# Decoder layer in one launch: the residual of cross attention's output put into the bank by TensorE for the halved batches, statistics and scaling read from the bank, and the last third put in another order

## The chip, the cores and the metric

The kernel runs on one core of one Trainium2 chip. The metric is the device time of one execution in microseconds, smaller is better. Engines are named as in the profile: PE is TensorE's matmul, PEld its weight load, DVE is VectorE, ACT is ScalarE, POOL is GpSimd, SP is SyncE, which issues the DMAs. "Bank" is one of the eight accumulator banks, 512 fp32 columns wide, that PE writes.

## The reference

The layer is a decoder block with the norm behind each residual. The input `x` is (4, 512, 128), the context (4, 77, 128), all fp32:

```python
x = _layernorm(x + _L0_attn_ref(x, ...))            # causal self attention, 16 heads of 64
x = _layernorm(x + _L0_xattn_ref(x, ctx, ctx, ...)) # cross attention, 16 heads of 8, 77 keys
x = _layernorm(x + _L0_ffn_ref(x, ...))             # one 128x128 GEMM on fp8-rounded inputs, bf16 result
```

`_layernorm` subtracts the mean over the 128 features and divides by the root of the variance plus 1e-5.

## The kernel before, in words

Each engine has its own list of instructions, and semaphores are set by hand. The first two thirds (`self_attention`) run 32 units of self attention, a pair of heads of one batch each. The last third (`rest_of_layer`) finishes the last unit and does the rest for the four batches (b = 0 to 3, 512 tokens or four tiles of 128 tokens each). Its order is written out by hand as a list of short calls, one list for each engine. It is these lists, and the table `USES`, that set the order of the work around the change.

A call is a piece. The pieces of PE, with the line that its rows carry in the profile:

- `scores(31, g)`, `sums(v)`, `weigh(v)`: the last units of self attention (L146 to L172).
- `y(b, i)`: output projection of self attention, tile i (L699). `t(b)`: transpose of the normed result (L679). `q(b)`: query projection (L712).
- `m(b, k)`: approximate scores, of which DVE takes maxima (L722), k = 0 to 7. `r(b)`: transpose of these maxima (L679).
- `s(b, k)`: exact scores of four of the sixteen heads, 77 keys x 512 queries each, into two double banks (L743), k = 0 to 3. ACT takes the exponential of each double bank in one instruction, so an `s` gives ACT two of them (L833).
- `p(b, part)`: values by probabilities (L756); it waits for ACT's exponentials of s(b, 2 part + 1). `o(b, part)`: its transpose (L679). DVE's `o` divides by the sums (L1012, L1016). `u(b)`: transpose of that (L679).
- `z(b)`: output projection of cross attention (L681). `x(b)`: transpose of the rounded input of the GEMM (L679). `f(b)`: the GEMM (L681).

ACT copies the banks of t, q, r, p, u and x to SBUF (all L807), takes the exponentials (L833), and has three pieces of the GEMM: `cast` (L854 and L856), `divide` (L860) and `f` (L873). POOL does `power` (L898, the inverse root of the variance) and its share of `scale` (L904, subtract the mean and multiply). DVE has `add` (L956 for norms 1 and 2, L946 and L950 for norm 3), `stats` (L967, L971, L974), its share of `scale` (L980), `m` (L1000), `q` (L989), `power_of_two` (L1026) and `fp8` (L1036 to L1042). For norms, `add(2, 3, "a")` is norm 2 of batch 3, first half.

Batches 2 and 3 go through the steps behind `u` in two halves, "a" (tiles 0 and 1) and "b" (tiles 2 and 3); 0 and 1 go whole.

Before the change, norm 2 of a half runs so: z writes the projection into a bank, `add(2, b, h)` on DVE adds the old value `xn` and writes `r_s` in SBUF, which frees the bank; `stats` reads `r_s`; POOL's `power`; then `scale` reads `r_s` and writes the new `xn`, on DVE for the first half and on POOL for the second. ACT's `cast` follows.

`USES` lists for each of five places (n0 and n1 are single banks, x0, x1 and x2 double ones) the pieces that use it, in order. A piece on PE first waits until the piece before it in that list has been taken out of the place (`claim`); then it fills it. PE's list is strictly in order, so a piece that waits holds back all that is behind it.

Of the kernel before, what the change touches and what calls it, by code (L numbers as in the profile page):

```python
# [1128 lines left out]
```

## Time and profile before

| what | us |
|---|---|
| median of 3 runs | 431.64 (429.62 to 431.91) |
| the profiled execution, its own time | 428.27 |
| its span in the profile | 426.5 |
| PE busy | 385.7 (90% of the span) |
| DVE busy | 307.5 (72%) |
| POOL busy | 239.8 (56%) |
| ACT busy | 237.6 (56%) |

The page of the profile first gives the busy time of each engine over the whole span. The shares hide that the stages differ, so the last third is read from rows in order of time (start, duration, engine, line, output and inputs, count, and in square brackets the idle time of the engine ahead of it with what ended it). Rows of one engine follow each other closely: an engine starts the next instruction a little before the last one's row ends, so the time that a piece takes of its engine is the difference between its start and the next one's.

### The profile page before, as it was taken

The numbers are of one execution on the slowest core, as the hardware profiler recorded it, in microseconds if no ns is written. First come the engines' busy times: TensorE is split into PE (matmuls) and PEld (weight loads), VectorE is DVE, ScalarE is ACT, GpSimd is POOL, SyncE is SP. The second block draws the span as 40 slices with busy tenths as digits, with TensorE's granted clock in tenths as the row PEclk, the third lists the DMA queues.
The fourth block names the chain that finished last, engine by engine and source line by source line (L and its number), as shares of the span: only waits on it lengthen the run. The fifth ranks groups of instructions, "written<-read, shape, count | busy, mean of one in ns | idle before, by whom it ended". The sixth has DMA issues, their size and how long they took to land.

```text
span 426.5 us, 9900 instructions
## 1 busy us (share of the span) xinstructions
PE 385.7 (90%) x3698; PEld 274.1 (64%) x3698; DVE 307.5 (72%) x924; ACT 237.6 (56%) x352; POOL 239.8 (56%) x338
## 2 busy tenths in 40 slices
PE   3779999999999999999999999799999999998821
PEld 1567666776767776677766767577787776544410
DVE  0646887877887777887788877976535655689897
ACT  2335665556665566665666556464512155788941
POOL 3466876556665565655667556465824430231775
PEclk9989999999999999999999999999999999999985
DMA  8012011000000300000000000000000000000001
GB/s 259 12 6 54 3 15 27 4 8 5 5 1 5 100 2 2 3 4 1 2 3 2 2 2 3 0 2 2 3 1 2 2 0 2 2 2 2 25 26 51
DMA packets 41568, 6.96 MB, mean 16 GB/s; under 512 B 38320, under 2 KB 40240, under 8 KB 41392
## 3 DMA queue, kind: packets, MB, share of 16 engines
q1 hardware_dynamic: 41520, 6.32, 9.3%
q8 instruction: 30, 0.49, 0.5%
q14 instruction: 18, 0.15, 0.1%
HBM read 5.12 MB, written 1.05 MB: 14 GB/s over the span
## 4 chain that ended last, share of the span: by engine, by line
PE 64%; DVE 14%; ACT 7%; DMA 7%; issue 4%; SPq 3%; POOLq 0%; POOL 0%; DVEq 0%; ACTq 0%
PE banks L172 11%; PE banks L146 10%; PE banks L214 8%; PE banks L699 7%; DMA shift<-neg_max 6%; PE banks L152 4%; PE banks L191 4%; DVE unused L352 3%; PE banks L130 3%; PE banks L743 3%; PE banks L165 3%; SPq L523 3%; PE banks L756 3%; ACT q_hi L305 2%; PE banks L163 2%
## 5 line engine op out<-in xcount | busy, mean ns | idle before, releaser
L286 ACT ACTIVATE probs<-banks 128x768 f32<-128x768 f32 (+1 forms) x96 | 84.9, 884 | 114.1 <-PE banks L152 114.1
L352 DVE CUSTOM_DVE_ANT_0 unused<-banks,neg_mask 128x512 bf16<-128x512 f32 (+3 forms) x256 | 112.6, 487 | 38.8 <-PE banks L130 38.8
L451 POOL TENSOR_SCALAR_AFFINE_SELECT probs<-probs 128x256 f32<-128x256 f32 x128 | 51.2, 412 | 112.7 <-ACT probs L286 111.3
L172 PE MATMUL banks<-probs,v_nat 128*64 128x256 f32 (+3 forms) x512 | 74.4, 433 | 0.0
L172 PEld LDWEIGHTS banks<-probs,v_nat 128*64 128x64 f32 x512 | 36.6, 137 | 45.3 <-issue 40.5
L152 PE MATMUL banks<-shift,ones_r 64*128 64x256 f32 (+3 forms) x256 | 42.9, 329 | 6.7 <-DMA shift<-neg_max 6.6
L898 POOL TENSOR_TENSOR rstd<-var_e,halves 128x4 f32<-128x4 f32 (+1 forms) x16 | 14.4, 898 | 60.1 <-DVE var_e L974 59.8
L146 PE MATMUL banks<-q_hi,k_hi 64*128 64x256 f32 (+3 forms) x256 | 43.5, 334 | 1.7 <-ACT probs L286 1.7
L361 DVE SCALAR_TENSOR_TENSOR q_lo<-banks,bias_qk,q_hi 128x512 fp32r<-128x512 f32 x32 | 24.0, 751 | 25.8 <-ACT q_hi L305 25.8
L146 PE MATMUL banks<-q_hi,k_lo 64*128 64x256 f32 (+3 forms) x256 | 41.9, 321 | 0.0
L146 PE MATMUL banks<-q_lo,k_hi 64*128 64x256 f32 (+3 forms) x256 | 41.8, 320 | 0.0
L477 POOL TENSOR_TENSOR p_sum<-probs 128x512 f32<-128x512 f32 x32 | 41.3, 1291 | 0.0
L485 POOL TENSOR_TENSOR p_sum<-p_sum,probs 128x512 f32<-128x512 f32 x32 | 41.1, 1283 | 0.0
L130 PE MATMUL banks<-k_hi,q_hi 64*128 64x512 f32 (+3 forms) x256 | 37.8, 331 | 2.6 <-ACT k_hi L305 1.5
L1000 DVE TENSOR_REDUCE top<-banks 128x8 f32<-128x616 f32 x32 | 25.1, 796 | 19.0 <-PE banks L722 18.9
L833 ACT ACTIVATE p_t<-banks 77x1024 f32<-77x1024 f32 x32 | 31.6, 1019 | 12.3 <-PE banks L743 12.3
L214 PE MATMUL banks<-x_hi,w_hi 64*128 64x512 f32 x128 | 27.1, 419 | 7.0 <-DVE x_lo L343 6.6
L152 PEld LDWEIGHTS banks<-shift,ones_r 64*128 64x128 f32 x256 | 24.7, 186 | 11.7 <-DMA shift<-neg_max 9.1
L699 PE MATMUL banks<-wo_s,attn_t 128*128 128x128 f32 x256 | 31.9, 279 | 0.0
L699 PEld LDWEIGHTS banks<-wo_s,attn_t 128*128 128x128 f32 x256 | 29.8, 192 | 2.6 <-issue 2.6
L146 PEld LDWEIGHTS banks<-q_hi,k_hi 64*128 64x128 f32 x256 | 24.4, 186 | 10.1 <-issue 5.3
L130 PEld LDWEIGHTS banks<-k_hi,q_hi 64*128 64x128 f32 x256 | 25.0, 190 | 8.4 <-issue 2.6
(125 smaller groups left out, 826.1 us busy)
## 6 DMA issues: line engine op xcount, KB each, us to landing
shift<-neg_max SPq DMA_DIRECT2D x256, 0.5 KB, 2.0
attn_t<-w_qkv SPq DMA_DIRECT2D x1, 1344.0 KB, 7.0
attn_t<-xT SPq DMA_DIRECT2D x4, 256.0 KB, 7.2
x_s<-x_nat SPq DMA_DIRECT2D x1, 1024.0 KB, 5.1
wo_s<-wo SPq DMA_DIRECT2D x1, 512.0 KB, 3.9
out<-y_out SPq DMA_DIRECT2D x2, 256.0 KB, 3.1
out<-y_out SPq DMA_DIRECT2D x4, 128.0 KB, 1.7
neg_mask<-causal SPq DMA_DIRECT2D x1, 256.0 KB, 3.8
```

The source lines that it names most:

```text
L130: last = mm(mx[:, h, at:at + n], q_hi[HALF[h], v % 3, i * T:(i + 1) * T], k_hi[HALF[h], v % 3, 0:n], start=True, stop=True)
L146: mm(st[:, h, at:at + n], k[HALF[h], par, ks], q[HALF[h], par, j * T:S], start=(c == 0), stop=False)
L152: last = mm(st[:, h, at:at + n], ones_r[HALF[h], :], shift[HALF[h], v % 2, j * T:S], start=False, stop=True)
L172: last = mm(o_ps[HALF[h], j * T:S], v_nat[:, v // 2 % 2, j, v % 2, HALF[h]], p_of(v, j, h, 0, S - j * T), start=(j == 0), stop=(j == NT - 1))
L214: last = mm(aux[qk], w[HALF[h], qk, p, :], x[HALF[h], xs], start=(part == 0 and c == 0), stop=(part == 1 and c == 2))
L286: nc.scalar.activation(probs[:, v % 2, AT[j]:AT[j] + 2 * n].rearrange("p (h s) -> p h s", h=2), st[:, :, 0:n], ACT.Exp, scale=D ** -0.5).t ...
L352: last = V.tensor_tensor_reduce(out=unused[:, h, at:at + n], in0=mx[:, h, at:at + n], in1=neg_mask[:, S - n:S], scale=-1.0, scalar=3.0e38, ...
L451: return nc.gpsimd.affine_select(out=blk, in_=blk, compare_op=ALU.is_ge, fill=0.0, base=0, pattern=pattern + [[1, T]], channel_multiplier=-1)
L477: nc.gpsimd.tensor_tensor(acc[:, :, T:], heads(1, T, 3 * T), heads(2, 0, 2 * T), ALU.add).then_inc(added, 1)
L485: nc.gpsimd.tensor_tensor(acc[:, :, T:], acc[:, :, T:], heads(0, 2 * T, S), ALU.add).then_inc(added, 1)
L699: last = mm(whole(bank)[:, i * T:(i + 1) * T], attn_t[:, p, at:at + T], wo_s[:, p, :], start=(p == 0), stop=(p == PAIRS - 1))
L833: nc.scalar.activation(p_t[:, k, 2 * half:2 * half + 2, :], place[bank][0:C, :, :], ACT.Exp, scale=DK ** -0.5).then_inc(taken[bank], 1)
```

## The change

1. A new piece `residual(b, h)` on PE, four times: it multiplies the identity by `xn` (256 columns, fp32) into the bank of z(b, h) with `start=True, stop=False`. z(b, h) then adds its projection to it in the bank (`start=False`).
2. DVE's `add(2, b, h)` is gone for the four halves. `stats` and `scale` of norm 2 read the bank itself; POOL can't do `scale` there, so DVE does all four. The bank counts as taken when `scale` is done.
3. `scale(1, 0)` and `scale(2, 1)` go from DVE to POOL.
4. All lists of the last third and `USES` are written in another order.

```diff
         SCALED:
-        "pool": "11 12 13 20 30 22b 31 23b 32a 32b", "dve": "10 21 22a 23a 33a 33b"
+        "pool": "10 11 12 13 20 21 30 31 32a 32b", "dve": "33a 33b"
...
+        def wait_scaled(eng, l, b, h=""):
+            if l == 2 and h:
+                wait_taken(eng, f"z{b}{h}")
+                return
...
+            def residual(b, h):
+                wait_scaled(pe, 1, b)
+                dst, _ = claim(f"z{b}{h}")
+                mm(dst[:, cols(h)], id_f[:, :], flat(xn, b, h), start=True, stop=False)
             def z(b, h=""):
                 wait_taken(pe, f"u{b}")
-                dst, done = claim(f"z{b}{h}")
-                four(dst, lambda i: on_t[:, i * T:(i + 1) * T], wx_s[:, 3, :], done, False, h)
+                if h:
+                    bank = BANK[f"z{b}{h}"][0]
+                    for i in TILES[h]:
+                        last = mm(whole(bank)[:, i * T:(i + 1) * T], on_t[:, i * T:(i + 1) * T], wx_s[:, 3, :],
+                                  start=False, stop=(i == TILES[h][-1]))
+                    last.then_inc(filled[bank], 1)
+                    return
...
 PE, from the last part of the list:
-            o(2, 0); m(3, 7); f(0); r(3); p(2, 1); s(3, 0); o(2, 1); s(3, 1); u(2); s(3, 2); x(1); z(2, "a")
-            z(2, "b"); s(3, 3); f(1); p(3, 0); p(3, 1); o(3, 0); o(3, 1); u(3); x(2, "a"); z(3, "a"); z(3, "b")
+            m(3, 7); o(2, 0); f(0); r(3); p(2, 1); s(3, 0); residual(2, "a"); o(2, 1); s(3, 1); u(2); z(2, "a")
+            x(1); s(3, 2); residual(2, "b"); f(1); z(2, "b"); s(3, 3); p(3, 0); p(3, 1); x(2, "a"); residual(3, "a")
+            o(3, 0); f(2, "a"); o(3, 1); x(2, "b"); f(2, "b"); u(3); z(3, "a"); residual(3, "b"); z(3, "b")
...
 DVE:
+            def summed(l, b, i, h):
+                if l == 2 and h:
+                    return whole(BANK[f"z{b}{h}"][0])[:, i * T:(i + 1) * T]
+                return r_s[:, b, i, :]
...
-                    last = V.bn_stats(out=stats_s[:, b, i, :], in_=r_s[:, b, i, :])
+                    last = V.bn_stats(out=stats_s[:, b, i, :], in_=summed(l, b, i, h))
...
-                    last = V.tensor_scalar((y_out if l == 3 else xn)[:, b, i, :], r_s[:, b, i, :], mv[:, b, i, 0:1],
+                    last = V.tensor_scalar((y_out if l == 3 else xn)[:, b, i, :], summed(l, b, i, h), mv[:, b, i, 0:1],
                                            rstd[:, b, i:i + 1], ALU.subtract, ALU.mult)
-                last.then_inc(dve_scaled, 1)
+                last.then_inc(taken[BANK[f"z{b}{h}"][0]] if l == 2 and h else dve_scaled, 1)
```

What the reordering does to three places on which the prediction rests follows as the lists of instructions of each kernel (line, operation, output and inputs, size, count). The lines of the changed kernel are numbered some 4 to 26 higher: L722 is L726 there, L743 is L747, L756 is L760, L679 is L683, L833 is L851, L807 is L825, L854 is L872, L1036 is L1062.

First, PE from z(0) to the first exact scores of batch 2. Before, `w_x_s,on_t` is z(0), `x_t,w_x_s` is q(3), and the first `q_hi,kx_hi 77x512` is s(2, 0):

```order
L681 MATMUL banks<-w_x_s,on_t 128x128 x4
L712 MATMUL banks<-x_t,w_x_s 128x512
L743 MATMUL banks<-q_hi,kx_hi 77x512 x4
L743 MATMUL banks<-q_lo,kx_hi 77x512 x4
L743 MATMUL banks<-q_hi,kx_lo 77x512 x4
L743 MATMUL banks<-shift,neg_sel 77x512 x4
```

And in the changed kernel:

```order
L685 MATMUL banks<-w_x_s,on_t 128x128 x4
L716 MATMUL banks<-x_t,w_x_s 128x512
L683 MATMUL banks<-ident_f_s,o_t 128x128 x4
L726 MATMUL banks<-kx_hi,q_hi 128x308 x4
L760 MATMUL banks<-p_t,vx 32x512 x8
L726 MATMUL banks<-kx_hi,q_hi 128x308 x4
L683 MATMUL banks<-ident_f_s,top 128x128 x4
L683 MATMUL banks<-ident_f_s,o_t 128x128 x4
L726 MATMUL banks<-kx_hi,q_hi 128x308 x2
L747 MATMUL banks<-q_hi,kx_hi 77x512 x4
```

Behind z(0) and q(3) there now stand o(1, 0), m(2, 6), m(2, 7), p(1, 1), m(3, 0), m(3, 1), r(2), o(1, 1) and m(3, 2) ahead of s(2, 0), which came at once before.

Second, ACT around the cast of batch 0 (L854 and L856, changed L872 and L874), before:

```order
L833 ACTIVATE p_t<-banks 77x1024 x2
L807 COPY o_t<-banks 128x512
L833 ACTIVATE p_t<-banks 77x1024 x2
L854 CAST x_b<-xn 128x512
L856 ACTIVATE qm<-x_b,sc 128x512
L860 ACTIVATE qv<-x_b,sc_r 128x512
L807 COPY on_t<-banks 128x512
```

and changed:

```order
L825 COPY o_t<-banks 128x512
L825 CAST shift<-banks 128x512
L872 CAST x_b<-xn 128x512
L874 ACTIVATE qm<-x_b,sc 128x512
L851 ACTIVATE p_t<-banks 77x1024 x2
L825 COPY on_t<-banks 128x512
L851 ACTIVATE p_t<-banks 77x1024 x2
L878 ACTIVATE qv<-x_b,sc_r 128x512
```

The four exponentials of s(2, 0) and s(2, 1), which stood ahead of the cast, now stand behind it. Near the end of ACT's exponentials the cast and the divide of batch 2's first half (L872, L874 and L878 on 128x256) now stand among them:

```order
L851 ACTIVATE p_t<-banks 77x1024
L872 CAST x_b<-xn 128x256
L874 ACTIVATE qm<-x_b,sc 128x256
L851 ACTIVATE p_t<-banks 77x1024
L878 ACTIVATE qv<-x_b,sc_r 128x256
L851 ACTIVATE p_t<-banks 77x1024
L825 COPY o_t<-banks 128x512
```

The last two exponentials there are those of s(3, 3), for which p(3, 1) waits; before, both casts came behind them.

Third, DVE around norm 2 of batch 3 (a `BN_STATS` on `banks` is of norm 2, one on `r_s` of norm 3), before:

```order
L956 TENSOR_TENSOR r_s<-banks,xn 128x256 x2
L967 BN_STATS stats<-r_s 128x6 x2
L971 BN_AGGR mv<-stats 128x2 x2
L974 TENSOR_SCALAR var_e<-mv 128x2
L967 BN_STATS stats<-r_s 128x6 x2
L971 BN_AGGR mv<-stats 128x2 x2
L974 TENSOR_SCALAR var_e<-mv 128x2
L946 TENSOR_TENSOR xq<-y_b,ffn_b_s 128x256
L950 TENSOR_TENSOR r_s<-xq,xn 128x256
L980 TENSOR_SCALAR xn<-r_s,mv,rstd 128x128 x2
```

and changed:

```order
L968 TENSOR_TENSOR r_s<-xq,xn 128x256
L993 BN_STATS stats<-r_s 128x6 x2
L997 BN_AGGR mv<-stats 128x2 x2
L1000 TENSOR_SCALAR var_e<-mv 128x2
L993 BN_STATS stats<-banks 128x6 x2
L997 BN_AGGR mv<-stats 128x2 x2
L1000 TENSOR_SCALAR var_e<-mv 128x2
L993 BN_STATS stats<-banks 128x6 x2
L997 BN_AGGR mv<-stats 128x2 x2
L1000 TENSOR_SCALAR var_e<-mv 128x2
L1006 TENSOR_SCALAR xn<-banks,mv,rstd 128x128 x2
```

The two adds from the bank are gone, and the two adds and the first statistics of norm 3 of batch 2 stand ahead of the statistics of batch 3.

## Rows read from the trace of the kernel before

**Rows 1.** The page: busy time, share of the span, instructions.

```profile
PE 385.7 (90%) x3698; PEld 274.1 (64%) x3698; DVE 307.5 (72%) x924; ACT 237.6 (56%) x352; POOL 239.8 (56%) x338
```

**Rows 2.** Busy time by stretch, core 0: length, then each engine's busy us.

```profile
381.40:391.10 9.70, 8.89 (x84) 4.20 (x82) 9.04 (x26) 7.66 (x12) 1.03 (x1) 1.00 0.00 1
391.10:404.20 13.10, 11.29 (x125) 5.34 (x121) 11.10 (x44) 12.45 (x19) 7.60 (x9) 1.00 0.06 21
404.20:426.50 22.30, 5.61 (x40) 3.17 (x36) 18.27 (x71) 8.10 (x19) 14.74 (x17) 0.70 0.11 37
```

**Rows 3.** PE in order of time, from z(0) to o(1, 1) and m(3, 2).

```profile
371.70 1.06 PE L681 MATMUL banks<-w_x_s,on_t 128*128 128x128 f32 x8
372.60 1.02 PE L712 MATMUL banks<-x_t,w_x_s 128*128 128x512 f32 x2
373.55 0.46 PE L743 MATMUL banks<-q_hi,kx_hi 32*77 32x512 f32 x4
...
374.54 0.32 PE L722 MATMUL banks<-kx_hi,q_hi 32*128 32x308 f32 x2
374.79 1.92 PE L756 MATMUL banks<-p_t,vx 77*32 77x512 f32 x16
376.64 0.41 PE L722 MATMUL banks<-kx_hi,q_hi 32*128 32x308 f32 x2
...
377.91 0.66 PE L679 MATMUL banks<-ident_f_s,o_t 128*128 128x128 f32 x4
378.50 0.41 PE L722 MATMUL banks<-kx_hi,q_hi 32*128 32x308 f32 x2
```

**Rows 4.** ACT and POOL in order of time, around the cast of batch 0.

```profile
377.99 1.93 ACT L833 ACTIVATE p_t<-banks 77x1024 f32<-77x1024 f32 x2 [0.57 <-PE banks L743]
379.81 0.61 ACT L854 CAST x_b<-xn 128x512 bf16<-128x512 f32 x1
...
381.09 0.71 ACT L860 ACTIVATE qv<-x_b,sc_r 128x512 f32<-128x512 bf16 x1
381.70 0.56 ACT L807 COPY on_t<-banks 128x512 f32<-128x512 f32 x1
...
376.23 3.13 POOL L904 TENSOR_SCALAR xn<-r_s,mv,rstd 128x128 f32<-128x128 f32 x4
```

**Rows 5.** PE in order of time: p(3, 1), u(3) and z(3).

```profile
402.34 1.92 PE L756 MATMUL banks<-p_t,vx 77*32 77x512 f32 x16 [0.39 <-ACT p_t L833]
...
406.59 0.66 PE L679 MATMUL banks<-ident_f_s,o_n 128*128 128x128 f32 x4 [0.91 <-DVE o_n L1016]
...
408.30 1.11 PE L681 MATMUL banks<-w_x_s,on_t 128*128 128x128 f32 x8
```

**Rows 6.** DVE in order of time, the last 17 us.

```profile
409.56 0.75 DVE L956 TENSOR_TENSOR r_s<-banks,xn 128x256 f32<-128x256 f32 x2
...
416.87 0.47 DVE L967 BATCH_NORM_STATS2 stats<-r_s 128x6 f32<-128x128 f32 x2
...
417.76 0.42 DVE L1036 SCALAR_TENSOR_TENSOR qv<-qm,qv 128x256 f32<-128x256 f32 x1
...
419.19 0.37 DVE L946 TENSOR_TENSOR xq<-y_b,ffn_b_s 128x256 bf16<-128x256 bf16 x1
419.60 0.43 DVE L950 TENSOR_TENSOR r_s<-xq,xn 128x256 f32<-128x256 bf16 x1
...
423.83 0.60 DVE L980 TENSOR_SCALAR y_out<-r_s,mv,rstd 128x128 f32<-128x128 f32 x2 [0.33 <-POOL rstd L898]
```

**Rows 7.** DVE by form from 355 us on: count, busy us, mean ns.

```profile
L1000 DVE TENSOR_REDUCE top<-banks 128x8 f32<-128x616 f32 x17 | 13.5, 796 | 5.6 <-PE banks L722 5.4
...
L956 DVE TENSOR_TENSOR r_s<-banks,xn 128x512 f32<-128x512 f32 x2 | 1.4, 686 | 0.5 <-PE banks L681 0.5
L1036 DVE SCALAR_TENSOR_TENSOR qv<-qm,qv 128x512 f32<-128x512 f32 x2 | 1.4, 681 | 0.0
...
L1026 DVE TENSOR_SCALAR qm<-qm 128x512 int32<-128x512 int32 x2 | 0.8, 423 | 0.4 <-ACT qm L856 0.4
```

More of the change, by code:

```diff
@@ L768, in u @@
                 four(dst, lambda i: o_n[:, i, :], id_f[:, :], done, True)
+            def residual(b, h):
+                wait_scaled(pe, 1, b)
+                dst, _ = claim(f"z{b}{h}")
+                mm(dst[:, cols(h)], id_f[:, :], flat(xn, b, h), start=True, stop=False)
             def z(b, h=""):
                 wait_taken(pe, f"u{b}")
[L773 to L774 removed]
+                if h:
[5 more added lines that the diff above has]
+                    return
+                dst, done = claim(f"z{b}")
+                four(dst, lambda i: on_t[:, i * T:(i + 1) * T], wx_s[:, 3, :], done)
             def x(b, h=""):
@@ L963, in stats @@
                     dve.wait_ge(r_out, ffn_at(b, h) + 1)
+                elif l == 2 and h:
+                    wait_filled(dve, f"z{b}{h}")
                 else:
@@ L1042, in fp8 @@
                 V.tensor_tensor(xq[:, b % 2, c], nan, neg, ALU.subtract).then_inc(quant_out, 1)
-            inverse(30); add(1, 0); stats(1, 0); normalise(30); scale(1, 0); m(0, 0); m(0, 1); m(0, 2); q(0)
-            add(1, 1); stats(1, 1); m(0, 3); inverse(31); normalise(31); m(0, 4); m(0, 5); m(0, 6); m(0, 7)
-            add(1, 2); stats(1, 2); q(1); m(1, 0); m(1, 1); m(1, 2); m(1, 3); m(1, 4); m(1, 5); m(1, 6); m(1, 7)
-            q(2); m(2, 0); add(1, 3); stats(1, 3); m(2, 1); m(2, 2); o(0, 0); m(2, 3); m(2, 4); m(2, 5); o(0, 1)
@@ L1049, in _ @@
-            m(2, 6); m(2, 7); o(1, 0); add(2, 0); stats(2, 0); m(3, 0); m(3, 1); q(3); o(1, 1); m(3, 2); m(3, 3)
-            power_of_two(0); m(3, 4); fp8(0); m(3, 5); add(2, 1); m(3, 6); stats(2, 1); m(3, 7); scale(2, 1)
-            o(2, 0); add(3, 0); power_of_two(1); stats(3, 0); o(2, 1); fp8(1); add(2, 2, "a"); add(2, 2, "b")
-            stats(2, 2, "a"); stats(2, 2, "b"); scale(2, 2, "a"); add(3, 1); stats(3, 1); power_of_two(2, "a")
-            power_of_two(2, "b"); o(3, 0); o(3, 1); fp8(2, "a"); fp8(2, "b"); add(2, 3, "a"); add(2, 3, "b")
@@ L1054, in _ @@
-            stats(2, 3, "a"); stats(2, 3, "b"); add(3, 2, "a"); scale(2, 3, "a"); stats(3, 2, "a"); add(3, 2, "b")
-            power_of_two(3, "a"); fp8(3, "a"); power_of_two(3, "b"); stats(3, 2, "b"); fp8(3, "b"); add(3, 3, "a")
-            stats(3, 3, "a"); add(3, 3, "b"); stats(3, 3, "b"); scale(3, 3, "a"); scale(3, 3, "b")
+            add(1, 0); inverse(30); stats(1, 0); normalise(30); inverse(31); add(1, 1); stats(1, 1); normalise(31)
+            m(0, 0); m(0, 1); m(0, 2); q(0); m(0, 3); m(0, 4); m(0, 5); m(0, 6); m(0, 7); q(1); m(1, 0); m(1, 1)
@@ new lines, in _ @@
+            add(1, 2); m(1, 2); stats(1, 2); m(1, 3); m(1, 4); m(1, 5); m(1, 6); m(1, 7); add(1, 3); stats(1, 3)
+            m(2, 0); o(0, 0); q(2); m(2, 1); m(2, 2); m(2, 3); o(0, 1); m(2, 4); m(2, 5); add(2, 0); stats(2, 0)
+            m(2, 6); q(3); m(2, 7); m(3, 0); o(1, 0); m(3, 1); m(3, 2); o(1, 1); m(3, 3); power_of_two(0); m(3, 4)
+            add(2, 1); stats(2, 1); m(3, 5); fp8(0); m(3, 6); m(3, 7); o(2, 0); add(3, 0); power_of_two(1)
+            stats(3, 0); o(2, 1); fp8(1); stats(2, 2, "a"); scale(2, 2, "a"); stats(2, 2, "b"); add(3, 1)
@@ L1059 @@
+            power_of_two(2, "a"); stats(3, 1); scale(2, 2, "b"); fp8(2, "a"); power_of_two(2, "b"); fp8(2, "b")
+            o(3, 0); o(3, 1); add(3, 2, "a"); add(3, 2, "b"); stats(3, 2, "a"); stats(2, 3, "a"); stats(2, 3, "b")
+            scale(2, 3, "a"); stats(3, 2, "b"); scale(2, 3, "b"); power_of_two(3, "a"); fp8(3, "a")
+            power_of_two(3, "b"); fp8(3, "b"); add(3, 3, "a"); stats(3, 3, "a"); add(3, 3, "b"); stats(3, 3, "b")
+            scale(3, 3, "a"); scale(3, 3, "b")
 _INS = ["xT", "w_qkv", "b_qk", "b_v", "causal", "ident", "x_nat", "wo", "b_o", "ctx_t", "w_x", "row_mask",
```

57 lines of the change are left out of this document (28 added, 29 removed), and 14 rows, old and new, of the table USES.

## The prediction

> **What bounds the kernel now.** The page's first line [rows 1] gives PE 90% of the span, the others 56 to 72%. As a share over all stages it says only where to begin. The next view is the busy time by stretch [rows 2]: from 391.1 to 404.2 us ACT is busy 12.45 of 13.10 us and PE 11.29, so in front of the end it is ACT that has no room. From 404.2 on PE has little work (5.61 of 22.3 us) and DVE is busy 18.27: the end is DVE's.
>
> The rows in order of time show where one takes over from the other. p(3, 1) starts at 402.34, released by ACT's last exponential, and takes 1.86 us, so PE is through with it at 404.20 [rows 5]. u(3) waits for DVE at 406.59, z(3) starts at 408.30 [rows 5], and what follows is DVE's queue until 424.43 [rows 6], a DMA and the end at 426.5. So I split the time in two: the end of p(3, 1) at 404.2, and a tail of 22.3 us. Each place of the change counts by which of the two it moves.
>
> **1. The late start of batch 2's scores.** Before, s(2, 0) follows z(0) and q(3): 371.70 to 373.55 [rows 3]. Now nine pieces stand in between. By rows 3 (start to start): z 0.90, q 0.95, two o and an r at 0.59 each, p 1.85, and five m at 0.34, of which a row of two matmuls gives the upper end 0.41: 7.2 us. Two of these pieces also wait for a double bank that a maximum of DVE must first leave; one maximum lasts 0.80 us [rows 7], and I take 0.6 for both (0 to 1.6). z(0) itself has o(1, 0), r(2), m(2, 6) and m(2, 7) no longer ahead of it, some 1.8 us, but waits ahead of it for two more maxima and ACT's banks; I take 1.6, so z(0) stays at 371.5. s(2, 0) then starts at about 379.3 instead of 373.55. PE loses nothing by that alone, since it does other work first. ACT does: eight exponentials of batch 2 instead of four now lie behind the cast of batch 0.
>
> **2. What that does to ACT.** The cast of batch 0 waits for the same chain as before, from z(0) through DVE's add and statistics and POOL's 3.13 us of scaling [rows 4]: it starts at about 379.3 and is through 1.28 us later (379.81 to 381.09 [rows 4]), at 380.6. From there to the exponential that p(3, 1) waits for, ACT's list holds 16 exponentials of 0.91 (two take 377.99 to 379.81 [rows 4]), 14.6 us; seven bank copies at 0.5 (0.56 by the row), 3.5; the second cast 1.28; two divides 0.61 each (381.09 to 381.70), 1.2; two pieces f, which no row here shows and which I put at a divide, 1.2; and now also the half cast and half divide of batch 2, at 0.64 to 1.28 and 0.3 to 0.6, taken as 0.9 and 0.4. Together 23.1 us: without any idle time ACT is through at 403.7. Before, ACT sat idle 2.04 and 0.65 us, 2.7 in all, over the two stretches in front of 404.2 [rows 2]. I take 2.4 now, since with more work behind it fewer waits are left, but z(2, "a") brings a new one (below). So ACT is through at 406.1 and p(3, 1) ends at 408.0: **3.8 us later**.
>
> **3. The residual matmuls.** q multiplies a 128x128 stationary with 512 fp32 columns in 0.95 us at most [rows 3]; 256 columns are half of it, some 0.45, four times 1.8 us of PE. Two lie ahead of s(3, 1) and f(1), where PE waits for ACT anyway; residual(3, "a") lies where the rest waits for DVE; residual(3, "b") holds up only z(3, "b"), which DVE reaches after 0.9 us of other statistics. Cost nothing; if that cover were gone, 1.8 us, the upper end. The lower end is nothing too: a matmul added gives nothing back.
>
> **4. The adds.** Four halves are gone, 0.33 us each (two take 409.56 to 410.3 less the overlap, 0.67 [rows 6]). Those of batch 2 are off the path, because p(3, 1) waits for ACT and not for them. Those of batch 3 count in the tail: **0.7 less**.
>
> **5. What DVE does ahead of z(3).** Two adds of norm 3 (0.41 and 0.43, with a gap 0.8 each: 419.19 to 420.03) and one half of its statistics (416.87 to 417.76, 0.9) [rows 6] now fill the time in which z(3) is still on its way; before they lay behind. **2.4 less**, if DVE is free by then. It should be: it waits for PE's transposes there.
>
> **6. What DVE gets in return.** scale of 3b comes from POOL: two tiles like those at 423.83, **0.6 more** [rows 6]. The way from p(3, 1) to z(3), 4.1 us before, has two more small matmul pieces in it: **0.2 more**.
>
> **7. Reading the bank.** DVE's add with a bank operand takes 0.686 us for 512 columns, the two-tensor operation from SBUF 0.681 [rows 7]: by these the bank costs nothing. But a tensor_scalar from SBUF takes 0.423 for the same columns [rows 7], and scale is of that kind. If from the bank it runs only as fast as the others, that is 0.26 for 512 columns, 0.065 for each of the four tiles of batch 3: **0.3 more**. I take it, being the row of the same operation; with the four tiles of batch 2, 0.5 is the upper end. The Trainium skill ("VectorE: DVE Perf Modes", section "Why PSUM operands drop a tier") speaks against the change here: an fp32 operation that reads PSUM runs one element per cycle, because the double rate needs both SBUF read ports. By the two equal rows alone the sum would be 0.3 lower; by the rule it is as I have it.
>
> **8. scale(1, 0) and scale(2, 1) to POOL.** A POOL scale takes 3.13 us [rows 4], DVE's four tiles 1.1. t(0) and the cast of batch 1 have that long to wait, and by my walk through the lists t(0) finds it just done and cast(1) comes 1 us behind it. Nothing; if t(0) is late, up to 1 us.
>
> **The sum.** 3.8 − 0.7 − 2.4 + 0.6 + 0.2 + 0.3 = **+1.8**: span 428.3, own time 428.27 + 1.8 = 430.1. The median of the runs shown stands 3.4 above the profiled execution, and I put the forecast there: 431.64 + 1.8 = **433.4 us**. This is 0.4%, and about 0.5% (2.2 us) is what a measurement of this kernel can tell from no change. With ACT's idle time from 1.2 to 2.7 us the forecast's own range is 432.2 to 433.7, and with the costs of parts 3, 7 and 8, 431.9 to 435.0.
>
> **The rivals.**
>
> *PE gets to z(0) early, and ACT never idles.* If the maxima don't hold PE up, z(0) comes at 369.9 and everything in part 2 is 1.6 us earlier; ACT at 402.1 without idle time, p(3, 1) ends at 404.0, and the tail is 20.3: −2.2, **429.4 us**. For it: PE was held up little before, 0.8 us of 9.7 without work in the stretch 381.4 to 391.1 [rows 2], with the same kinds of pieces. Against it: in the stretches shown ACT was never without idle time [rows 2].
>
> *ACT's waits swallow it.* ACT had 2.7 us of idle time; if the additional work only fills that (0.8 us left), then +0.2, **431.8 us**, and the whole change is a move of waits that does nothing for the time.
>
> *z(2, "a") holds PE up, and with it ACT.* This one is slower. z(2, "a") now stands directly behind u(2). It needs ACT's copy of u(2), which stands in ACT's list behind both exponentials of s(3, 1). By my walk PE waits 1.5 us there, and x(1), s(3, 2), residual(2, "b"), f(1), z(2, "b") and s(3, 3) wait behind it; before, s(3, 2) and x(1) came ahead of z(2). If ACT runs dry for that, its idle time is 2.7 + 1.5 = 4.2, p(3, 1) ends at 409.8, and it comes out at +3.6: **435.2 us**. It decides from 2.8 us of idle time on (that is +2.2). For it: PE has nothing left to do between u(2) and z(2, "a"). Against: when u(2) comes, ACT still has two exponentials in hand.
>
> **How the numbers follow.** Forecast 0.37, of which 0.03 lies above +0.5%; the waits swallow it 0.13, 0.02 of it below −0.5%; early z(0) 0.18; z(2, "a") 0.32. So faster 0.20, same 0.45, slower 0.35. The range 428.5 to 436.5 leaves out half of the early case and the far third of the z(2, "a") case, 0.1 each.
>
> **What would show it.** In the profile of the changed kernel: s(2, 0) at 379 and not 374; the cast of batch 0 through at 380 to 381 and ACT nearly without a gap behind it; a PE wait of 1 to 1.5 us ahead of the half z(2, "a"); p(3, 1) starting at 406, released by ACT; the span's end 20.3 us behind the end of p(3, 1); residual rows of two matmuls in 0.45; scale from the bank at 0.06 a tile more than from r_s. I am wrong if p(3, 1) ends within 1 us of 404.2, or if the tail is not near 20 us, or if t(0) waits for POOL.

## The result and the profile after

The changed kernel takes **436.12 us** (median of 4 runs, 434.79 to 436.58), the kernel before, on the same chip, 430.63 (4 runs, 429.50 to 431.91): a ratio of **1.0129** (95% interval 1.0093 to 1.0165), 5.5 us or 1.3% slower. The profiled execution of the changed kernel has an own time of 435.78 us and a span of 433.7, against 428.27 and 426.5 before. The forecast was 433.4 with a range of 428.5 to 436.5, so the time lies in the range, but near its end, and the likeliest case (within 0.5% of before) was not what came. The sum of the parts said +1.8 us, and it is +5.5. That the time still lies in the range is in part luck: the forecast counted from 431.64 for the kernel before, which came out at 430.63 here, and as a difference the range ended at +4.9.

The page's first line, which answers to [rows 1]:

```profile
PE 389.0 (90%) x3706; PEld 277.5 (64%) x3706; DVE 304.9 (70%) x916; ACT 238.0 (55%) x352; POOL 242.8 (56%) x342
```

The shares are within two points of those of before, so again they only say where to begin. The busy time by stretch of the changed kernel (length, then PE, PEld, DVE, ACT and POOL, the granted clock of TensorE, DMA), with cuts at the places of the prediction:

```profile
305.00:310.00 5.00, 4.76 (x27) 3.96 (x28) 1.88 (x5) 1.93 (x3) 1.76 (x3) 0.66 0.00 0
...
374.00:384.00 10.00, 8.95 (x78) 4.90 (x74) 7.30 (x19) 5.23 (x9) 4.16 (x5) 1.00 0.01 2
384.00:391.00 7.00, 6.47 (x78) 4.03 (x82) 5.08 (x17) 6.97 (x10) 0.00 (x0) 1.00 0.01 2
391.00:401.00 10.00, 8.96 (x98) 4.51 (x90) 8.55 (x24) 8.66 (x14) 5.70 (x6) 1.00 0.00 0
401.00:407.50 6.50, 4.95 (x58) 3.29 (x54) 4.51 (x17) 5.84 (x8) 2.62 (x5) 1.00 0.01 3
...
412.80:433.70 20.90, 6.17 (x44) 4.01 (x40) 16.75 (x65) 7.09 (x16) 10.56 (x13) 0.72 0.11 38
```

Two things are to be seen. From 374 to 384 ACT is busy 5.23 of 10 us: it waits for its first work of batch 2, as forecast. And in the first row, long before any of that, the granted clock is 0.66, a mean of the two levels 1.0 and 0.5 (2.4 and 1.2 GHz); in the same stretch of before it is 1.00. That place was not in the prediction at all. In order of time, PE of the changed kernel at the start of the last third:

```profile
302.34 0.39 PE L146 MATMUL banks<-q_hi,k_hi 64*128 64x256 f32 x2
...
305.24 0.44 PE L163 MATMUL banks<-probs,ones 128*64 128x128 f32 x4 [1.77 <-DVE attn_t L399]
305.48 1.08 PE L165 MATMUL banks<-p_sum,ones 128*64 128x384 f32 x4
306.49 5.76 PE L703 MATMUL banks<-wo_s,attn_t 128*128 128x128 f32 x37
```

and the same of before:

```profile
301.10 0.39 PE L146 MATMUL banks<-q_hi,k_hi 64*128 64x256 f32 x2
...
302.16 2.05 PE L699 MATMUL banks<-wo_s,attn_t 128*128 128x128 f32 x16
304.14 0.44 PE L163 MATMUL banks<-probs,ones 128*64 128x128 f32 x4
304.41 0.81 PE L165 MATMUL banks<-p_sum,ones 128*64 128x384 f32 x4
305.16 2.05 PE L699 MATMUL banks<-wo_s,attn_t 128*128 128x128 f32 x16
```

The first rows of the two are scores(31, 0), in code that the change doesn't touch. Behind it before has y(0, 0) (16 matmuls of L699) and then sums(30). The change's list has sums(30) first, and sums(30) overwrites banks that DVE must have left (attn_t, L399): PE now waits **1.77 us**. In before that wait is there too, only y(0, 0) lies in it. After it the clock goes to its lower level: L165 takes 1.01 us start to start instead of 0.75, and the 37 matmuls of wo in this row take 5.76 us, where before 16 take 1.98 start to start, which makes 4.6 for 37. That is **1.4 us** more, by rows at either level.

PE of the changed kernel at the places that the prediction names (s(2, 0); then, from 403, z(2, "a"), residual(2, "b"), p(3, 1) and z(3, "a")):

```profile
383.97 0.46 PE L747 MATMUL banks<-q_hi,kx_hi 32*77 32x512 f32 x4 [0.57 <-DVE top L1026]
...
403.25 0.71 PE L786 MATMUL banks<-w_x_s,on_t 128*128 128x128 f32 x4 [1.07 <-ACT on_t L825]
405.20 0.70 PE L778 MATMUL banks<-xn,ident_f_s 128*128 128x256 f32 x2
...
410.97 1.92 PE L760 MATMUL banks<-p_t,vx 77*32 77x512 f32 x16 [0.86 <-ACT p_t L851]
...
417.63 0.71 PE L786 MATMUL banks<-w_x_s,on_t 128*128 128x128 f32 x4 [0.73 <-ACT on_t L825]
```

p(3, 1) starts at 410.97 against 402.34 in before [rows 5], released by ACT's last exponential as before. The span ends 22.7 us behind that start, before 24.2.

**A yardstick for one profile against another.** The untouched code ahead of scores(31, 0) is not equally long in all executions: its start lies at 301.10 in before, at 302.34 here, and between 301.3 and 304.7 in the other kernels (the table below). So places of the last third are compared by their distance from scores(31, 0). By that, p(3, 1) is 7.4 us later than in before, and the whole last third 6.0 us longer.

### The profile page after: what moved, and what is told of

The parts are those of the page before. It is cut to its first block, busy times and chain, and to the rows that moved or that the text cites. A ratio compares the mean times of both kernels' runs of the same rounds, so it can differ in the third digit from the quotient of the medians.

```text
span 433.7 us, 9912 instructions
## 1 busy us (share of the span) xinstructions
PE 389.0 (90%) x3706; PEld 277.5 (64%) x3706; DVE 304.9 (70%) x916; ACT 238.0 (55%) x352; POOL 242.8 (56%) x342
## 3 DMA queue, kind: packets, MB, share of 16 engines
HBM read 5.12 MB, written 1.05 MB: 14 GB/s over the span
## 4 chain that ended last, share of the span: by engine, by line
PE 57%; DVE 14%; ACT 9%; DMA 8%; SPq 5%; issue 4%; POOL 1%; POOLq 0%; DVEq 0%; ACTq 0%
PE banks L172 10%; PE banks L146 9%; DMA shift<-neg_max 7%; PE banks L703 7%; PE banks L214 7%; SPq L523 5%; PE banks L152 4%; DVE unused L352 4%; PE banks L191 4%; PE banks L130 3%; PE banks L165 3%; PE banks L747 3%; ACT q_hi L305 2%; PE banks L760 2%; PE banks L163 2%
## 5 line engine op out<-in xcount | busy, mean ns | idle before, releaser
L851 ACT ACTIVATE p_t<-banks 77x1024 f32<-77x1024 f32 x32 | 31.3, 1015 | 12.2 <-PE banks L747 12.2
L703 PEld LDWEIGHTS banks<-wo_s,attn_t 128*128 128x128 f32 x256 | 30.8, 199 | 2.9 <-issue 2.6
```

Source lines behind the costliest of these rows:

```text
L703: last = mm(whole(bank)[:, i * T:(i + 1) * T], attn_t[:, p, at:at + T], wo_s[:, p, :], start=(p == 0), stop=(p == PAIRS - 1))
L851: nc.scalar.activation(p_t[:, k, 2 * half:2 * half + 2, :], place[bank][0:C, :, :], ACT.Exp, scale=DK ** -0.5).then_inc(taken[bank], 1)
```

## The experiments

All times are medians, the ratio (of the runs, with its 95% interval; it is not the ratio of the two medians to the last digit) is to before on the same chip; before stood at 429.88 us (21 runs) beside e1 to e4, 429.75 (27) beside e5 to e8, 429.57 (29) beside e9 to e11 and 431.18 (17) beside e12. The last three columns are of the profiled executions: the start of scores(31, 0), and from there to the start of p(3, 1) and to the end of the span.

| kernel | us (runs) | ratio, 95% | start | to p(3, 1) | to the end |
|---|---|---|---|---|---|
| before | 430.63 (4) | 1 | 301.10 | 101.2 | 125.4 |
| the change | 436.12 (4) | 1.0129 (1.0093 to 1.0165) | 302.34 | 108.6 | 131.4 |
| e1: y(0, 0) ahead of sums(30) | 433.44 (8) | 1.0079 (1.0048 to 1.0111) | 301.36 | 106.3 | 128.9 |
| e2: the change's order, adds | 437.62 (5) | 1.0178 (1.0135 to 1.0221) | 303.96 | 108.6 | 132.3 |
| e3: before's front, the change's end | 432.51 (11) | 1.0070 (1.0044 to 1.0097) | 303.56 | 104.7 | 127.3 |
| e4: e3 with adds | 433.89 (8) | 1.0090 (1.0056 to 1.0123) | 301.56 | 104.6 | 128.3 |
| e5: e3, scale(2, 1) on DVE | 431.18 (11) | 1.0031 (1.0006 to 1.0056) | 304.06 | 102.9 | 125.5 |
| e6: e5, cast(2, "a") behind the exponentials | 434.02 (5) | 1.0102 (1.0063 to 1.0142) | 301.88 | 102.2 | 130.3 |
| e7: e5, z(2, "a") behind s(3, 2) | 431.11 (11) | 1.0043 (1.0018 to 1.0068) | 301.29 | 103.3 | 126.7 |
| e8: e5, s(3, 2) and s(3, 3) earlier in PE's list | 432.38 (11) | 1.0074 (1.0049 to 1.0098) | 302.87 | 102.5 | 127.8 |
| e9: residual, order near before's | 432.95 (12) | 1.0083 (1.0055 to 1.0112) | 303.96 | 104.1 | 129.7 |
| e10: before, sums(30) first | 431.86 (12) | 1.0046 (1.0020 to 1.0073) | 301.49 | 102.9 | 127.6 |
| e11: e5 with adds | 431.31 (12) | 1.0041 (1.0018 to 1.0063) | 301.71 | 102.9 | 127.1 |
| e12: e7, s(3, 2) ahead of x(1) | 432.42 (12) | 1.0023 (1.0000 to 1.0046) | 304.70 | 103.0 | 126.0 |

### e1: y(0, 0) ahead of sums(30) again

```diff
-            scores(31, 0); sums(30); y(0, 0); y(1, 0); y(0, 1); scores(31, 1); y(0, 2); y(1, 1); y(0, 3)
+            scores(31, 0); y(0, 0); sums(30); y(1, 0); y(0, 1); scores(31, 1); y(0, 2); y(1, 1); y(0, 3)
```

Expected:

> The changed kernel with one swap on PE: y(0, 0) again ahead of sums(30), as before the change. In the changed kernel's profile PE waits 1.77 us ahead of sums(30) for DVE's L399 of unit 29, which y(0, 0) covered before. If the wait is paid in full at the end (PE has no idle time behind it until 334), the time falls by 1.5 to 1.8 us, to 1.009 of the kernel before. The rival: something later in the stretch is late anyway (POOL's scale(1, 0), which t(0) waits for, or DVE's L399 of unit 31), and takes the time back: then less than 0.5 us is gained and a new PE wait stands ahead of t(0) or of m(0, 2).

Measured: 2.7 us less than the change, and by the ratios 0.50% or 2.2 us. The row of s(2, 0) in e1:

```profile
379.77 0.72 PE L747 MATMUL banks<-q_hi,kx_hi 32*77 32x512 f32 x4 [0.57 <-DVE top L1026]
```

From scores(31, 0) it stands at 78.4 us, in the changed kernel at 81.6: 3.2 us for a swap of two pieces, which is the 1.77 of the wait and the 1.4 of the lower clock behind it. So a wait of PE costs more than its length where the clock falls behind it.

That p(3, 1) then comes only 2.3 us earlier (106.3 against 108.6) has a reason in e1's own profile. Its row above takes 0.72 us, the same four matmuls in the changed kernel 0.46: behind the wait of 0.57 us the clock is at its lower level here too, for some 3 us, and behind the same wait in the changed kernel it is not. The transposes shortly behind it, first in e1, then in the changed kernel:

```profile
381.96 1.12 PE L683 MATMUL banks<-ident_f_s,o_n 128*128 128x128 f32 x4
```

```profile
385.20 0.66 PE L683 MATMUL banks<-ident_f_s,o_n 128*128 128x128 f32 x4
```

From s(2, 0) to z(1) e1 takes 4.54 us and the changed kernel 3.70, which is the missing 0.8.

### e10: the same swap in the kernel before

```diff
-            scores(31, 0); y(0, 0); sums(30); y(0, 1); scores(31, 1); y(0, 2); context(); y(0, 3); weigh(30)
+            scores(31, 0); sums(30); y(0, 0); y(0, 1); scores(31, 1); y(0, 2); context(); y(0, 3); weigh(30)
```

Expected:

> Before, with nothing moved but y(0, 0) from ahead of sums(30) to behind it on PE. The wait ahead of sums(30) was 1.77 us in the changed kernel and gone in e1, which was 2.7 us faster. Theory 'PE's time here goes to the end in full': 1.8 to 2.7 us above before, 431.5 to 432.4. Rival 'the middle has idle time that swallows it in the order of before': within 0.7 us of before.

Measured: 2.3 us above before, by the ratio 2.0. The row of sums(30) in e10:

```profile
304.39 0.44 PE L163 MATMUL banks<-probs,ones 128*64 128x128 f32 x4 [1.77 <-DVE attn_t L399]
```

The same 1.77 us, and here the clock stayed at its higher level up to 407 us. The last third is 2.2 us longer than before's (127.6 against 125.4), 1.6 of it ahead of p(3, 1). So the wait goes to the end in full, in either kernel, and the middle does not swallow it. This is the firmer of the two measurements of the swap: its interval (0.20 to 0.73%, 0.9 to 3.1 us) does not reach zero, while the intervals of the change and of e1 overlap.

### e2, e4 and e11: adds in place of the residual

Each is its partner (the change, e3, e5) without the residual matmuls, DVE adding the half of xn as before; the scales of the four halves stay on DVE and read r_s. The edit on DVE, as in e11:

```diff
-            fp8(1); stats(2, 2, "a"); scale(2, 2, "a"); stats(2, 2, "b")
+            fp8(1); add(2, 2, "a"); stats(2, 2, "a"); scale(2, 2, "a"); add(2, 2, "b"); stats(2, 2, "b")
```

Expected:

> The changed kernel's order of all lists, but with norm 2 of the halves as before the change: no residual matmuls, DVE adds xn from SBUF to the bank, statistics and scaling read SBUF (scaling of all four halves stays on DVE). It measures what the residual in the bank is worth in its own order. If DVE's queue is full from the first exponential's end to the end, the two adds of batch 3 cost 2 x 0.33 us in the tail, less 0.25 us for the scaling that reads SBUF again: the time rises by 0.4 to 0.7 us over the changed kernel (ratio to before 1.014). The rival is that the residual is itself the loss (four matmuls of 0.5 us on PE, banks held until scale is done): then it is 1 us or more faster than the changed kernel (1.010 or less).

> As the kernel with the front as before and the change's end, but with norm 2 of the halves by DVE adds as before the change (no residual matmuls, scaling of all four halves on DVE from SBUF). With the other three it makes a table of two fronts by two ways of adding. The effect of the residual in the bank should be the same with either front: this one 0.4 to 0.7 us slower than the one with the residual. If the residual is the loss, it is 1 us or more faster.

> e5 with DVE's adds in place of the residual: before's front and scale(2, 1) on DVE, so that against before only the order of the end is new. Theory 'the residual is worth 1.4 us and the end's order costs what is left': 1.4 us above e5, 432.6, 2.8 above before. Rival 'the scale of batch 1 and not the order made e4 slow': within 0.7 us of before.

Measured, adds less residual: e2 less the change +0.49%, e4 less e3 +0.20%, e11 less e5 +0.10%, that is 2.1, 0.9 and 0.4 us; by the distance from scores(31, 0) to the end 0.9, 1.0 and 1.6. Each pair's intervals overlap, but all six signs agree: the residual in the bank is a gain of about 1 us, and not what makes the change slow. The profiles show where: in e2 and e4 the way from p(3, 1) to z(3, "a") takes 7.04 us, with the residual 6.66, and from z(3, "a") to the end 16.7 against 16.0 to 16.1. In e11 PE's clock also fell early in the tail (0.65 from 411 to 413, at its higher level at the same place in e5), and its way to the end is 0.5 longer still. The 1.4 us that I expected of e11 did not show in its median (0.13 us), so by the runs the size stays open between 0.4 and 2. e11 against before is the change's end without the residual, that is its new order, its table of banks, and scale(2, 2, "b") and scale(2, 3, "b") on DVE: 1.0041, which is 1.8 us slower (1.7 by the profiles, all of it ahead of p(3, 1)). Which of these makes it was not separated.

### e3 and e5: the front of the last third, and one scale

e3 has before's lists on every engine up to r(3) on PE and m(3, 7) on DVE, and the change's end; scale(1, 0) is on DVE again, scale(2, 1) on POOL. e5 moves that one too:

```diff
-        SCALED = {"pool": "11 12 13 20 21 30 31 32a 32b".split(), "dve": "10 33a 33b".split()}
+        SCALED = {"pool": "11 12 13 20 30 31 32a 32b".split(), "dve": "10 21 33a 33b".split()}
...
-            m(3, 6); stats(2, 1); m(3, 7); o(2, 0)
+            m(3, 6); stats(2, 1); m(3, 7); scale(2, 1); o(2, 0)
```

Expected:

> The change's end with the front of the last third as before: all lists and the table of banks of the kernel before up to r(3) on PE, f(0) and r(3) on ACT, m(3, 7) on DVE and power(2, 1) on POOL; behind these the changed kernel's lists, with the residual in the bank. My theory puts the loss into the front (sums(30), the late s(2, 0) and the waits around it) and a gain of 1.4 us into the tail: p(3, 1) then ends within 1.5 us of the kernel before, the tail stays at 20.9 us or less, and the time is 0.996 to 1.002 of before. The rival puts the loss into the change's end (z(2, a) right behind u(2), casts between the exponentials of s(3, 3), residual matmuls): then p(3, 1) ends 3 us or more later than before and the time is 1.006 or more.

> The kernel with the front as before and the change's end, and scale(2, 1) back on DVE as before the change. In the profile without this, ACT sat idle 2.32 us ahead of the cast of batch 1 for POOL's L920 (3.21 us), DVE 2.88 us behind it and PE 1.37 us ahead of o(2, 1). If POOL's slower scaling is what the moved scale(2, 1) costs there, p(3, 1) ends 1.5 to 2.1 us earlier and the time is 1.002 to 1.004 of before. If DVE, which now does the four tiles in 1.1 us, is what matters then, or the casts between the exponentials hold p(3, 1) anyway, the gain is less than 0.7 us.

Measured: e3 1.0070, which is 0.4 us less than e1: apart from sums(30), the change's front can't be told from before's. e5 1.0031, another 1.7 us less (1.3 by the medians, 1.8 by the distance to the end; the two intervals still overlap). In e3, ACT and POOL:

```profile
391.55 3.21 POOL L920 TENSOR_SCALAR xn<-r_s,mv,rstd 128x128 f32<-128x128 f32 x4
```

```profile
394.79 0.62 ACT L870 CAST x_b<-xn 128x512 bf16<-128x512 f32 x1 [2.32 <-POOL xn L920]
```

ACT stands 2.32 us waiting for POOL's scaling of four tiles, which DVE does in 1.1, and DVE waits behind ACT. In the changed kernel the cast at the same place has no wait in its row:

```profile
396.82 0.63 ACT L872 CAST x_b<-xn 128x512 bf16<-128x512 f32 x1
```

There ACT came late for other reasons: the exponentials of batch 2 that now stand behind the cast of batch 0. It isn't sums(30), because in e1 the same cast (393.46) has no wait either. So the move of scale(2, 1) costs where the front is before's, and seems hidden with the change's. What it costs in the changed kernel itself was not run.

### e6: the casts behind the exponentials

```diff
-            f(1); s(3, 2, 1); cast(2, "a"); s(3, 3, 0); divide(2, "a"); s(3, 3, 1); p(3, 0)
+            f(1); s(3, 2, 1); s(3, 3, 0); s(3, 3, 1); cast(2, "a"); divide(2, "a"); p(3, 0)
```

Expected:

> As e5_scale_back, with ACT's cast(2, a) and divide(2, a) behind the last exponential of s(3, 3), as before the change. They take 1.25 us of ACT in front of it. If they hold up p(3, 1), it ends 1.2 us earlier, and the time falls by 0.5 to 1.2 us, since in the tail DVE's fp8(2, a) starts later. If DVE's queue sets the end and not p(3, 1), the time rises by up to 0.7 us instead, although p(3, 1) ends earlier.

Measured: 1.0102, 3.0 us slower than e5 by the ratios. By the distance from scores(31, 0) p(3, 1) does come 0.7 us earlier, but the end 4.8 later. DVE in e6, and PE behind p(3, 1):

```profile
404.91 0.29 DVE L1050 TENSOR_SCALAR qm<-qm 128x256 int32<-128x256 int32 x1 [2.26 <-ACT qm L872]
```

```profile
404.09 1.92 PE L758 MATMUL banks<-p_t,vx 77*32 77x512 f32 x16 [0.16 <-ACT p_t L849]
408.80 0.39 PE L681 MATMUL banks<-ident_s,xq 128*128 128x128 bf16 x2 [2.78 <-DVE xq L1066]
408.99 1.17 PE L776 MATMUL banks<-xn,ident_f_s 128*128 128x256 f32 x2
409.94 1.06 PE L681 MATMUL banks<-ident_f_s,o_t 128*128 128x128 f32 x4
```

The same rows of e5:

```profile
406.93 1.92 PE L758 MATMUL banks<-p_t,vx 77*32 77x512 f32 x16 [0.84 <-ACT p_t L849]
408.79 0.29 PE L681 MATMUL banks<-ident_s,xq 128*128 128x128 bf16 x2
408.91 0.65 PE L776 MATMUL banks<-xn,ident_f_s 128*128 128x256 f32 x2
409.39 0.60 PE L681 MATMUL banks<-ident_f_s,o_t 128*128 128x128 f32 x4
```

The change put power_of_two(2, "a") ahead of stats(3, 1) in DVE's list. With the cast late DVE stands 2.26 us in front of it with stats(3, 1) behind, PE then waits 2.78 for DVE, and after that PE's clock is at its lower level for the rest (o_t 1.06 us instead of 0.60). By stretch, first e6 then e5, from p(3, 1) to z(3):

```profile
404.10:414.90 10.80, 6.68 (x39) 4.08 (x39) 8.54 (x31) 5.68 (x13) 4.61 (x5) 0.65 0.13 49
```

```profile
406.90:413.60 6.70, 4.83 (x39) 2.55 (x39) 6.22 (x20) 4.42 (x10) 4.36 (x5) 1.00 0.12 44
```

The same 39 matmuls of PE (the count of the rows), 10.8 against 6.7 us, waits and lower clock together. My thought that the half cast holds up p(3, 1) and so the end was half right: 0.7 us of p(3, 1), and worth far less than what DVE gets by it.

### e7, e8, e12: what stands between u(2) and p(3, 1)

```diff
 e5:   u(2); z(2, "a"); x(1); s(3, 2); residual(2, "b"); f(1); z(2, "b"); s(3, 3)
 e7:   u(2); x(1); s(3, 2); z(2, "a"); residual(2, "b"); f(1); z(2, "b"); s(3, 3)
 e8:   u(2); s(3, 2); x(1); z(2, "a"); f(1); s(3, 3); residual(2, "b"); z(2, "b")
 e12:  u(2); s(3, 2); x(1); z(2, "a"); residual(2, "b"); f(1); z(2, "b"); s(3, 3)
```

Expected:

> As e5_scale_back, with z(2, a) on PE behind x(1) and s(3, 2), not right behind u(2). PE waited 1.0 us ahead of z(2, a) for ACT's copy; s(3, 2) can start in that time. If this wait holds up ACT's exponentials and p(3, 1), the time falls by 0.5 to 1 us. If ACT has work in hand there, or s(3, 2) then waits as long for its bank or x(1) for fp8(1), the time stays within 0.3 us and the statistics of 2a come 1 us later.

> As e5_scale_back, with two changes of order: PE runs s(3, 2), x(1), z(2, a), f(1), s(3, 3), residual(2, b), z(2, b), and f(1) writes into n0 instead of x1, so that s(3, 3) no longer waits for ACT's f(1) (0.47 us) nor z(2, a) for ACT's copy (1.0 us); ACT has f(1) behind the exponentials of s(3, 2). If PE's waits in front of s(3, 3) are what makes p(3, 1) late, the time falls by 1 to 1.5 us and reaches or beats the kernel before (0.997 to 1.001). If ACT is full there, p(3, 1) moves by less than 0.5 us.

> e7 with s(3, 2) ahead of x(1) on PE, as before has it, and the matching order on ACT (both exponentials of s(3, 2) around x(1), f(1) behind). In e7 PE waited 1.32 us ahead of x(1) for DVE's xq, and s(3, 2) takes 1.08 us of PE and needs nothing of that wait. Theory 'p(3, 1) is set by PE's waits here': 0.7 to 1.1 us less than e7, 430.0 to 430.4, and then within 0.7 us of before. Rival 'ACT's list and DVE's queue set it': no change against e7, 431.1, or slower if f(1), now copied behind both exponentials, holds up s(3, 3).

Measured: e7 the same as e5, e8 1.8 us slower than e5 by the ratios, e12 between before and e5 (1.0023, its interval begins at 1.0000). In e7 the wait ahead of z(2, "a") is gone, and this one stands in its place:

```profile
396.69 0.40 PE L681 MATMUL banks<-ident_s,xq 128*128 128x128 bf16 x4 [1.32 <-DVE xq L1066]
```

So "z(2, a) holds PE up" is not a cost of its own: whatever piece stands there waits for ACT or DVE. e12 fills that wait with s(3, 2); its ratio to before is 0.2% less than e7's (the medians give 0.03%), and its last third 0.7 us shorter by the profiles, which is the size expected but inside the intervals. e8, which also puts f(1) into another bank, brings p(3, 1) 0.4 us earlier and loses 2.7 behind it (25.3 us to the end against 22.6), where z(2, "b") comes after s(3, 3). As in e6, PE waits there for DVE and then has the lower clock; the granted clock from 407.5 to 410 is 0.73:

```profile
407.50:410.00 2.50, 0.98 (x4) 0.87 (x5) 2.23 (x7) 1.79 (x5) 2.40 (x4) 0.73 0.00 0
```

```profile
409.02 0.40 PE L681 MATMUL banks<-ident_s,xq 128*128 128x128 bf16 x2 [1.71 <-DVE xq L1066]
```

### e9: the residual in an order near before's

On DVE before's order to the end (stats(3, 1) ahead of the power of two), on ACT the casts of batch 2 behind the last exponential as before; scale of the four halves on DVE from the bank. The residual stands close ahead of its z, only residual(3, "a") directly behind p(3, 1). It is not before's order everywhere: on PE x(1) stands ahead of s(3, 2) and f(1) ahead of s(3, 3), ACT's list is changed to match, and the table of banks is the change's. On DVE against before:

```diff
-            fp8(1); add(2, 2, "a"); add(2, 2, "b"); stats(2, 2, "a"); stats(2, 2, "b"); scale(2, 2, "a"); add(3, 1)
+            fp8(1); stats(2, 2, "a"); stats(2, 2, "b"); scale(2, 2, "a"); scale(2, 2, "b"); add(3, 1)
```

Expected:

> The residual alone, in the order of before: ACT's and DVE's lists to the end as before (casts of batch 2 behind the last exponential, power of two of batch 2 behind stats(3, 1)), with the residual by TensorE, statistics and scaling from the bank, f(1) ahead of s(3, 3) for the banks' sake. Theory 'the residual is a gain of 1.4 us in any order': 1.4 us less than before, and 0 to 1 us back for the banks that are held until scaling and not until the add (p(3, 1) stood 1.0 us later against scores(31, 0) in e6 than before): 428.4 to 429.4, ratio 0.997 to 0.999. Rival 'only the order of the change has room for it': DVE reaches scale(2, 3, a) and (2, 3, b) late in this order, batch 3's cast with them, and it is 1 us or more above before, 430.8 on.

Measured: 1.0083, 3.6 us slower than before; the rival was right in sign, for a reason that neither theory named. PE in e9:

```profile
399.63 0.40 PE L681 MATMUL banks<-ident_s,xq 128*128 128x128 bf16 x4 [1.58 <-DVE xq L1066]
...
401.40 1.22 PE L776 MATMUL banks<-xn,ident_f_s 128*128 128x256 f32 x2
402.42 1.06 PE L784 MATMUL banks<-w_x_s,on_t 128*128 128x128 f32 x4
```

With x(1) ahead of s(3, 2), and z(2, "a") and f(1) behind both, PE waits 1.58 us for DVE, and from about 400.8 to 404 residual and z run at the lower clock. DVE has then nothing to do for 3.94 us until z(2, "a") is there:

```profile
403.51 0.49 DVE L991 BATCH_NORM_STATS2 stats<-banks 128x6 f32<-128x128 f32 x2 [3.94 <-PE banks L784]
```

In this order, then, DVE gets its bank late. That the residual needs an order that gives DVE its bank early is argued from these rows and not shown: neither this order with adds nor the residual with before's places of x(1) and f(1) was run. No kernel that was run is faster than before.

## Why the prediction was right or wrong

**The account of the 5.5 us**, by ratios: sums(30) ahead of y(0, 0) 2.2 (the change less e1; 2.0 in e10); the rest of the front 0.4 (e1 less e3); scale(2, 1) on POOL 1.7 in before's front (e3 less e5); the end's new order 1.8 (e11); the residual −0.4 (e5 less e11). Unrounded they make the 1.29% of the whole, and they must: each is the difference of two neighbours in one chain of kernels from the change to before, so their sum checks nothing. By the intervals of the ratios each is uncertain by 1 to 2 us (an estimate). The 2.2 is backed by e10 and the 1.8 by e11, each compared with before directly and clear of zero; the 1.7 is clear of it only barely, and the 0.4 and −0.4 are not. On another path the steps would differ: the third was measured in a front that the changed kernel doesn't have.

**Part 1, the start of s(2, 0): the step that failed.** I walked the list from z(0) on and kept z(0) at 371.5, without going through the front of the list, where sums(30) changes its place with y(0, 0). s(2, 0) was forecast at 379.3 and came at 383.97. Of the 4.7 us, 1.2 lie ahead of scores(31, 0), in code that is the same; 1.8 are the wait; 1.4 the lower clock behind it; 0.2 is left. In e1, without wait and clock, s(2, 0) stands at 379.77, and 379.5 with its own start put to before's. From z(0) to s(2, 0) it is 7.8 us in both kernels, as forecast, but two errors cancel in it: the waits for the two maxima are 1.05 us (0.48 and 0.57 in the rows) where I had 0.6, and the pieces are shorter by as much. In these profiles the term that was missing is 3.2 us; what it is worth in the time is less sure, 2.2 us by the runs (e1; 2.0 in e10), of the 3.7 between +1.8 and +5.5. The profiles, in which the last third is 6.0 us longer and not 5.5, give the rest as 0.2 at s(2, 0), 0.2 from there to p(3, 1) and 0.6 in the tail.

**Part 2, ACT: right.** From the end of the cast of batch 0 to the exponential that p(3, 1) waits for I had 23.1 us of work and 2.4 idle; it is 385.23 to 410.9, 25.7 us, of which ACT is busy 23.6 and idle 2.0. The cast waited for POOL (0.65 us), through the same chain:

```profile
383.95 0.62 ACT L872 CAST x_b<-xn 128x512 bf16<-128x512 f32 x1 [0.65 <-POOL xn L922]
```

Counted from scores(31, 0) the cast's end is 3.4 us later than forecast, 3.2 of them for part 1's reason; p(3, 1), forecast to start at 406.1, started at 410.97, which is 3.6 by the same count.

**Part 3, the residual matmuls: right.** Their rows read 0.60 to 0.70 for two, not the 0.45 that I named as a sign, but the next piece starts 0.44 to 0.54 behind; PE had room for them, and in sum the residual was a gain (e2, e4, e11).

**Parts 4 to 6, the tail: one term short.** Forecast 2.0 shorter (with part 7), measured 1.4. From z(3, "a") on it is 2.1 shorter (16.1 us against 18.2), which is what the adds, the work ahead of z(3) and the scales made together (−2.2). The kernels with adds split it: e2 and e4 take 16.7 us there, so the order and the moved scales give 1.5 (parts 5 and 6 had 1.8) and the residual and the bank 0.6 (parts 4 and 7 had 0.4). The way from p(3, 1) to z(3) was costed 0.2 longer and is 0.7 (417.63 less 410.97 is 6.66, before 5.96).

**Part 7, reading the bank: right.** DVE in the changed kernel, statistics and scaling from the bank, then the scale from r_s:

```profile
404.00 0.50 DVE L993 BATCH_NORM_STATS2 stats<-banks 128x6 f32<-128x128 f32 x2 [0.79 <-PE banks L786]
...
405.80 0.73 DVE L1006 TENSOR_SCALAR xn<-banks,mv,rstd 128x128 f32<-128x128 f32 x2 [0.81 <-POOL rstd L916]
...
417.37 0.48 DVE L993 BATCH_NORM_STATS2 stats<-r_s 128x6 f32<-128x128 f32 x2
...
430.01 0.60 DVE L1006 TENSOR_SCALAR y_out<-r_s,mv,rstd 128x128 f32<-128x128 f32 x2
```

0.73 against 0.60 us for two tiles is 0.065 a tile, as taken from the nearest row. With the rule of the Trainium skill that the prediction names ("VectorE: DVE Perf Modes", "Why PSUM operands drop a tier": an fp32 operation with a PSUM operand gets no double rate) the trace agrees for this operation. The statistics cost the same from either (0.50 and 0.48).

**Part 8, the scales on POOL: right for the changed kernel, and for a reason that I didn't see.** t(0) and cast(1) show no wait for POOL there. With before's front ACT waits 2.32 us (e3), and the move costs 1.7. What hid it in the changed kernel is ACT's additional work behind the cast of batch 0, and not the wait at sums(30): in e1, without that wait, the cast of batch 1 has no wait either.

**The rivals.** Early z(0) did not happen: counted from scores(31, 0) z(0) starts at 70.6 us in e1, as in before. That the waits swallow it did not either: ACT's idle time stayed, 2.0 us. "z(2, a) holds PE up" came nearest in the number (435.2), but its mechanism is not what made the time: the wait is there with 1.07 us where I had 1.5, and moving z(2, "a") out of it changed nothing that the runs can tell (e7). The range reached up to 436.5 for this rival's sake, so that the measured time lies in it is luck and not this mechanism. The rival that would have been right was one I didn't have: a wait at the far front of the moved list, and the clock behind it.

## What to carry to other kernels

When an order is rewritten, walk all of it and not only around the operation that the change is about: here the residual was a gain of about 1 us, and one swap of two pieces, some 95 us ahead of the first residual matmul, cost about 2. For each piece that has lost its neighbour ask what wait that neighbour covered; a wait of the busiest engine that shows in no row of before because work lies in it is still there. And price a new wait of PE above its length where it may bring the lower clock.
